# Cross-attention and FFN on one core: the quad preparation and the FFN scales move behind VectorE's softmax chain

## The reference

```
x = x + xattn(layernorm(x), ctx)       # 16 heads of 128
    q = (x @ Wq) / sqrt(128);  k = ctx @ Wk;  v = ctx @ Wv
    softmax(q k^T) v, then @ Wo
x = x + ffn(layernorm(x))              # 512 -> 2048 -> 512
    q_act, q_w: MX quantisation in blocks of 32 along the last axis
    gate = q_act(x) @ q_w(w_gate)^T;  up = q_act(x) @ q_w(w_up)^T
    q_act(silu(gate) * up) @ q_w(w_down)^T
```

## Time and profile before

| | us |
|---|---|
| median of 3 runs | 2310.7 (2306.71 to 2312.22) |
| profiled execution | 2307.97 |
| its span | 2306.4 |
| busy: PE, DVE, ACT, POOL | 2138.5, 1636.6, 1135.3, 778.4 |
| attention, about | the first 1800 |
| FFN, about | the last 500 |

### The profile page before, as it was taken

One profiled execution on the slowest core, in us unless ns is written; L12 is line 12 of the kernel. 1 busy time (PEld: TensorE's weight loads), 2 busy tenths in 40 slices (PEclk: granted clock), 3 DMA queues, 4 the chain that ended last, 5 costly groups with the idle time before them and its releaser, 6 DMA issues.

```text
span 2306.4 us, 51300 instructions
## 1 busy us (share of the span) xinstructions
PE 2138.5 (93%) x16458; PEld 1555.5 (67%) x16458; DVE 1636.6 (71%) x3487; ACT 1135.3 (49%) x3016; POOL 778.4 (34%) x1156
## 2 busy tenths in 40 slices
PE   6999999999999999999999999999998888888887
PEld 5677777777777777777777777777886433333333
DVE  6766666666666666666666666655554699999998
ACT  7754444444454444444444444544444444454443
POOL 4322222222232222222222222211100367666674
PEclk9999999999999999999999999999999999999999
DMA  6723323232323232333332333232324211111111
GB/s 221 184 64 74 78 63 83 65 79 64 80 63 79 65 79 60 79 67 79 65 82 64 79 64 80 54 70 60 58 58 115 78 52 53 55 50 50 55 50 46
DMA packets 321374, 170.75 MB, mean 74 GB/s; under 512 B 277504, under 2 KB 290304, under 8 KB 321216
## 3 DMA queue, kind: packets, MB, share of 16 engines
q1 hardware_dynamic: 304720, 129.81, 25.5%
q0 software_dynamic: 10320, 32.25, 4.6%
q10 hardware_dynamic: 6176, 6.29, 0.9%
HBM read 77.86 MB, written 23.07 MB: 44 GB/s over the span
## 4 chain that ended last, share of the span: by engine, by line
PE 53%; DVE 26%; issue 10%; DMA 5%; ACT 5%; DVEq 1%; POOL 0%; POOLq 0%; SPq 0%; ACTq 0%
PE b_qk L1038 18%; PE b_v L1038 11%; PE b_w L1148 6%; PE b_c L1038 6%; PE b_s L1038 6%; DMA probT<-psplit 5%; PE b_o L1148 4%; DVE psplit L818 4%; DVE attn_weights L950 3%; ACT psplit L590 3%; DVE attn_weights L965 3%; DVE attn_weights L955 3%; DVE ffn_amax L761 2%; DVE x_amax L880 1%; DVE rsum L812 1%
## 5 line engine op out<-in xcount | busy, mean ns | idle before, releaser
L582 ACT ACTIVATE prob<-b_s,nmax 128x256 f32<-128x256 f32 x514 | 238.8, 469 | 510.3 <-DVE nmax L802 509.8
L818 DVE SCALAR_TENSOR_TENSOR psplit<-prob,rrec,psplit 128x256 f16<-128x256 f32 x514 | 252.8, 533 | 266.1 <-ACT psplit L590 266.1
L1038 PE MATMUL b_qk<-xT,attn_weights 128*128 (+1 forms) x3072 | 379.9, 274 | 0.0
L1038 PE MATMUL b_v<-attn_weights,kvT 128*128 128x256 f16 x3072 | 378.6, 273 | 0.0
L1038 PE MATMUL b_qk<-kvT,attn_weights 128*128 (+1 forms) x3072 | 377.8, 273 | 0.0
L590 ACT ACTIVATE psplit<-prob,rrec 128x256 f16<-128x256 f32 x514 | 233.2, 500 | 226.1 <-DVE rrec L815 223.7
L1038 PEld LDWEIGHTS b_qk<-xT,attn_weights 128*128 128x128 f16 x3072 | 301.5, 98 | 36.3
L1038 PEld LDWEIGHTS b_v<-attn_weights,kvT 128*128 (+1 forms) x3072 | 301.1, 98 | 35.5
L1038 PEld LDWEIGHTS b_qk<-kvT,attn_weights 128*128 128x128 f16 x3072 | 300.8, 98 | 35.4
L802 DVE TENSOR_REDUCE nmax<-b_s 128x2 f32<-128x512 f32 x257 | 177.0, 689 | 116.1 <-PE b_s L1038 115.9
L391 POOL DMA_DIRECT2D kvrow<-kvt x61 | 34.7, 569 | 628.5 <-DVE kvT L727 628.5
(11 more groups left out here) (133 smaller groups left out, 3197.4 us busy)
## 6 DMA issues: line engine op xcount, KB each, us to landing
ffn_w<-wffn SPq DMA_DIRECT2D x48, 256.0 KB, 2.7
acc<-xtok POOLq DMA_DIRECT2D x16, 512.0 KB, 4.3
x_tiles<-x_scratch SPq DMA_DIRECT2D x32, 256.0 KB, 2.7
attn_weights<-x_scratch SPq DMA_DIRECT2D x32, 256.0 KB, 2.6
out<-attn_weights SPq DMA_DIRECT2D x32, 256.0 KB, 2.0
xrow<-xq POOLq DMA_DIRECT2D x61, 128.0 KB, 2.5
kvrow<-kvt POOLq DMA_DIRECT2D x61, 128.0 KB, 2.3
x_scratch<-acc POOLq DMA_DIRECT2D x15, 512.0 KB, 3.3
```

The lines of the kernel that those rows point to most:

```text
L582: last = eng.activation(half(prob, q, 256), half(bS, q, 256), ACT.Exp, bias=nmax[:, q:q + 1], scale=1.0, accum_out=rsum[:, q:q + 1])
L818: last = eng.scalar_tensor_tensor(out=p_part(k, q, 1), in0=half(prob, q, 256), scalar=rrec[:, q:q + 1], in1=p_part(k, q, 0), op0=ALU.mult, ...
L1038: last = eng.matmul(out, l, r, start=(a == 0), stop=(a == len(pairs) - 1))
```

## The change

VectorE's extra tasks all move behind the head's last low half (vbuf): x_stats and ffn_scales at the end of head 0; x_apply, kv_lo and ffn_y at the end of head 1; x_lo at the end of head 2. So x_lo and kv_lo have changed heads, and with them ScalarE's x_prep and kv_prep. TensorE's x_transpose moves from head 1 to head 2. GpSimd's and SyncE's code is as it was.

```diff
--- before.py
+++ after.py
@@ -596,9 +596,9 @@
                     if front:
                         hi(half(vbuf, 2 * k, 256), bV[:, 0:256], V_OUT, "v_done", i + 1, "v_hi")
                     if prepare and k == 1:
+                        kv_prep(n)
+                    if prepare and k == 2:
                         x_prep(n)
-                    if prepare and k == 2:
-                        kv_prep(n)
                     if ffn and k == 0:
                         w = n - FFN_FROM - 1
                         eng.wait_ge(sm["ffn_tr"], w + 1)
@@ -801,12 +801,6 @@
                         eng.wait_ge(sm["s_done"], i + 1)
                         eng.tensor_reduce(nmax[:, :], bS[:, :].rearrange("p (q f) -> p q f", q=2), AX_X, ALU.max,
                                           negate=True).then_inc(sm["max_done"], 1)
-                    if prepare and k == 0:
-                        x_stats(n)
-                    if prepare and k == 1:
-                        x_apply(n)
-                    if ffn and k == 0:
-                        ffn_scales(w)
                     if front or k == 0:
                         eng.wait_ge(sm["exp_done"], i + 1)
                         eng.tensor_scalar(rsum[:, :], rsum[:, :], 1.0 / P_SCALE, None, ALU.mult
@@ -821,18 +815,23 @@
                         last.then_inc(sm["p_lo"], 1)
                     if front:
                         lo(half(qk, 1), bQK[:, :], half(qk, 0), QK_OUT, "qk_hi", i + 1, "qk_lo")
-                    if ffn and k == 1:
-                        ffn_y(w)
                     if front or k < 2:
                         s = 2 * ((k + 2) % 4)
                         lo(half(cbuf, s + 1, 256), bC[:, 0:256], half(cbuf, s, 256), C_OUT, "c_hi", i + 1, "c_lo")
                     if front:
                         lo(half(vbuf, 2 * k + 1, 256), bV[:, 0:256], half(vbuf, 2 * k, 256), V_OUT,
                            "v_hi", i + 1, "v_lo")
+                    if prepare and k == 0:
+                        x_stats(n)
+                    if ffn and k == 0:
+                        ffn_scales(w)
                     if prepare and k == 1:
+                        x_apply(n)
+                        kv_lo(n)
+                    if ffn and k == 1:
+                        ffn_y(w)
+                    if prepare and k == 2:
                         x_lo(n)
-                    if prepare and k == 2:
-                        kv_lo(n)
                     if isinstance(n, int) and n == NQ and k == 3:
                         inner(0, 0)
 
```

## The result

The changed kernel takes 2463.93 us (median of 4 runs) against 2309.41: ratio 1.067, 95% interval 1.065 to 1.068, 154.5 us slower. I had forecast 2392, 82 us slower, with a range of 2320 to 2405.

What follows compares the result with a forecast made beforehand. TensorE, 97.6% busy, was taken to bound the attention stage, waiting only for VectorE's chain. FFN quads +78.5, batch ends +2.4 and startup +1.3 gave +82 us, so 2392; range 2320 to 2405.

Steps and rivals of the forecast that it cites:

- What bounds the kernel, and the 1.0 us a head can lose: Attention stage: TensorE bounds; VectorE's loop is 5.55 of a 6.54 us head, so 1.0 us can go before TensorE waits.
- b_s of head 1 is on time: Head 0 of an FFN quad: stats and scales leave the chain, so head 1's scores start at 6.76; 0.36 stall goes.
- all in series: Head 1: the tasks behind qk_lo run one after another, so head 2's maximum starts at 16.49, against 14.46.
- the term c: Head 2: what GpSimd's rounding adds to VectorE's chain; taken as 1.78 us, bounds 0 and 1.9.
- an offset of .29, under the limit: Head 2: L431 starts .29 us behind the maximum, under about .41, so rsum waits for L433's end.
- Rival (a): Head 2: GpSimd comes later, rsum slips in front of L433; +15 to +40 us, 2325 to 2350; chance .33.
- Sum over the quads, 48 x 29.51: FFN quads: 48 x (27.73 + 1.78) = 1416.5 us, less 1337.95, is +78.5 us.
- I charge .2: Batch ends, 12 of 48 quads: the first accumulation delays head 3's maximum; .2 us each, bounds 0 and .7, 2.4 together.
- The first four quads, +1.3: Startup quads that also split weights: psplit waits may go or stats and apply add; bounds -3 and +6, middle +1.3 us.
- Quads without FFN and the tail: The 7 preparing quads behind the FFN quads, and the tail: nothing changes, nothing is moved.

Runs made afterwards that it cites:

- e4: Kernel before the change with only ffn_scales moved behind v_lo in head 0: 2288.2 us, ratio 0.9907.
- e6: Kernel before the change with only x_stats and ffn_scales moved behind v_lo of head 0: 2323.4 us, ratio 1.0054.
- e1: Changed kernel, but GpSimd rounds an FFN tile only after VectorE has written the psplit of head 2: 2342.9 us, ratio 1.0145.
- e9: Changed kernel, but GpSimd starts rounding only when VectorE has finished the maximum of head 2: 2366.0 us, ratio 1.0253.
- e5: Changed kernel with x_stats and ffn_scales back between the maximum and the sums of head 0: 2387.4 us, ratio 1.0333.
- e2: Changed kernel with 16 additional matmuls on TensorE ahead of head 3's scores in quads 5 to 52, filling its stall: 2431.7 us, ratio 1.0530.
- e7: Changed kernel with TensorE's loop over the FFN batches written out: 2448.5 us, ratio 1.0592.
- e10: Kernel before the change with TensorE's loop over the FFN batches written out, nothing else: 2320.0 us, ratio 1.0051.
- e3: Changed kernel with the tasks of quads 0 to 3 back in their old places on all engines: 2454.7 us, ratio 1.0624.

## Why the prediction was wrong, step by step

- *What bounds the kernel, and the 1.0 us a head can lose:* right. e4 (1.9 us behind v_lo, TensorE waits for qk once in 48 quads) and e6 (2.7 us, no gain) lie on either side of it.
- *Head 0, "b_s of head 1 is on time":* right. The maximum of head 1 starts 740.75 - 732.63 = 8.12 behind that of head 0; from 8.91 - .85 = 8.06 were forecast. The stall before head 2 is 738.53 + 6.54 to 745.48 = .41 (forecast .31).
- *Head 1, all in series:* right. The maximum of head 2 came 7.56 behind that of head 1 (forecast 16.49 - 8.91 = 7.58).
- *Head 2 and the term c, "an offset of .29, under the limit":* right, .31 and 1.74. The reason given was rsum alone; .70 of the 1.74 is psplit, which came in unnamed with the c of rows 7. (In the quads of rows 8 it is nearly all of c: psplit takes 1.23, .35 more.) e1 and e9 show that it is GpSimd's rounding, and that half a microsecond decides. Rival (a) was off here only because the loads do run back to back; when e9 moves L431 past the limit, its c of .57 is what (a) described. (a) also leaned on the Trainium skill, "SBUF — State Buffer", section "SBUF: two separate sides", by which GpSimd can't write a DMA's descriptors while VectorE is in a two-port mode. The loads did not hold L431 back: .65 and .57 us beside the passes, against .63 and .57. But their data came later, 4.0 and 3.6 us from issue to landing in the median of the whole execution against 2.5 and 2.3 before. Whether late descriptors are the cause or the other transfers beside them, no run here shows.
- *Sum over the quads, 48 x 29.51:* **this is the step that failed.** It took every matmul behind the stall at the time that it has in the FFN quads of before. After a stall of 2.07 us TensorE's granted clock fell, and the next two groups took 4.29 us from start to start in place of 2.62. It fell neither behind stalls of 1.2 to 1.5 us (e5) nor where the stall was filled (e2), which gave 34 us back. The FFN quads of before had no stall this long (1.6 at most) and a clock of 1.00, so none of the rows that I read warned of it. The trace did, in its startup, of which the prediction names no row of TensorE: the 2.81 us stall shown above. The prediction foresaw a stall longer than any that its prices came from, and kept those prices.
- *Quad ends, "I charge .2":* wrong term. The accumulation costs .1 at most (29.66 in e7); the end of TensorE's loop costs 1.2 to 2.0 us, ten times, once no VectorE wait covers it. Before, TensorE waited there for VectorE's chain, and writing the loop out left these quads as they were (e10). e7 took 15 us off.
- *The first four quads, +1.3:* mis-sized, +13.2. I followed the moved tasks on VectorE and asked of GpSimd only about rounding. Its queue stands at x_apply ahead of the weight splits, the SP queue stands at these splits, and the next head's transposing DMA stands behind SP's reloads. That the moved tasks of quads 0 to 3 cost this is shown by e3; the chain through the queues is read from the trace. e5 shows that the late x_apply is enough for 10 of the 13 us, e6 that late statistics cost as much by another chain.
- *Quads without FFN and the tail:* right, +0.6 us together.

The profiled executions lie 153.9 us apart, 71.7 more than the 82.2 of the forecast. The clock is 33.9 of it (e2), the batch ends without the clock 18.0 (20.4 in e2 against 2.4), the startup 11.9, what else the ordinary quads lose in e2 5.4, 29.55 for 29.51 us 2.0, and the rest .6. That c and the quad came out within .1 us was not luck: c was taken from the nearest collision in the trace, and the heads came out as reckoned.

## What to carry to other kernels

Work put "behind" a chain is free only up to the gap there plus the slack of the next chain; measure both and move only as much (here 1.9 us fitted and gave 22 us, 2.7 gave nothing, the whole change lost 154). When a step is moved, walk every queue that is released by it and ask what it now runs beside: an operation of .17 us that meets another engine's pass can take 1.2. And when a forecast contains a TensorE stall longer than any in the stage that its prices come from, the matmuls behind it must not be priced at the old clock; look through the whole trace for a stall of that length.

## What the runs showed of the hardware that I had not expected

- Stalls of 2.07 us in an otherwise busy TensorE were followed by matmul groups at 1.2 GHz in 14 of 36 ordinary quads (2.31 for 1.47 us) and not in the other 22; those of 1.2 to 1.5 us (e5) and of .8 to 1.0 (e9) were followed by none. Single longer ones went either way too: 2.27 us (e10) and 2.81 (before) were followed by slow groups, 2.53 (before) was not. What decides between them stays open. The Trainium skill, "TensorE: Matmul & The Clock Gate", section "Part 1: The HAM clock gate", has a gate that halves the clock by how busy TensorE has been; that it fell only behind stalls here agrees.
- The end of TensorE's loop shows as 1.2 to 2.0 us of idle time without a releaser (ten times in the changed kernel, none in e7) when no wait for VectorE covers it.
- GpSimd's two DMA-issuing instructions kept their times beside VectorE's .43 us passes (.65 and .57 us), and the passes kept theirs, but the median from issue to landing was 4.0 and 3.6 us in place of 2.5 and 2.3.
